# Attention and a two-of-eight expert layer on one core: one tag per token, a wait gone from the row scatters, and VectorE's low halves one position on

## The chip, the cores and the metric

The kernel runs on one core of a Trainium2 chip. The metric is the device time of one execution in microseconds, and less is better. The engines are named TensorE (PE in the profile), VectorE (DVE), ScalarE (ACT), GpSimd (POOL) and SyncE (SP, which here only issues transfers). Each engine runs its own instructions in the order in which they are written, and waits on semaphores for the others.

## The reference, cut to what matters

Eight sequences of 512 tokens with 256 channels pass an attention block, and the 4096 tokens then pass a shared feed-forward network and two of eight expert networks each.

```python
x = layernorm(x + attention(x))                    # 16 heads of 16, causal, q and k normed and rotated
normed = x * rsqrt(mean(x*x) + 1e-8) * norm_weight
shared = relu(normed @ sw1 + sb1) @ sw2 + sb2      # 256 -> 1024 -> 256
probs = sigmoid(normed @ router_w.T)               # 8 experts
scores, idx = top_k(probs, 2)
w = scores / (sum(scores) + 1e-6)
routed = sum over the two chosen e of  w_e * (relu(normed @ ew1[e] + eb1[e]) @ ew2[e] + eb2[e])
x = layernorm(x + shared + routed)
```

## The kernel before

**Two halves.** The first half runs a schedule of positions g from -33 to 209. A sequence c takes 20 positions more than the one before; tables of offsets (`QN`, `NAT`, `PROJ`, `NORMS`, `XN_ROWS`, `SCATTER` and others) say at which position of its sequence a piece of work stands, and `due(offsets, g)` lists what stands at g. Every engine has its own `step(g)`, which fixes the order inside a position. Nothing reorders anything: the tables and the lines of `step` are the order. The second half runs 39 routed tiles and 10 late tiles of the shared network.

**The attention part.** TensorE makes q, k and v (L1511), GpSimd rotates halves (`swap`, L629 and L632) and copies the normed q and k (`nat_high` L641, `nat_twice` L648 and L649), VectorE does the rest around these (`summed` L1069, `normed` L1084, `nat_low` L1094). TensorE computes scores (L1480), ScalarE exponentiates (L806), TensorE multiplies by v (L1502) and turns the result back (`NAT`, L1632, into the PSUM bank `mb`). VectorE then divides by the row sums (`averaged`: L1102 reads the sums, L1103 divides, and with that `mb` is free for the next `NAT`). `PROJ` (L1644) is the output projection, `added` (L1121) the residual, `norms` and `shifted` (L658 to L668 and L688 on GpSimd) the norms, `normalised` (L1143 to L1147) splits the normed rows into an fp16 high and low part in `xnh`.

**Routing.** `chosen` finds each token's two experts, `ranked` the row that each copy of the token gets in the list `xg_rows`, sorted by expert. Then GpSimd scatters: `scatter(c, t, k)` sends the 128 rows of tile t of sequence c to their row for the first (k = 0) or second (k = 1) expert with one indirect transfer (L679). Each row carries a tag in a column of `xnh`, written right ahead by a memset (L677), that tells row and k; the tag of k = 1 overwrites that of k = 0, so `scatter` with k = 1 waits until the four transfers with k = 0 have landed. There are 64 scatters, eight per sequence.

**Early tiles.** Six tiles of 256 tokens of the shared network (`N_EARLY`) are done at positions 161 to 206, beside the last sequence. A tile m has two hidden halves (`H`, L1564) and two output halves (`O`, L1601). ScalarE applies the ReLU of a hidden half at the next position (`early_hidden`, L861 and L865), VectorE makes its low half `hh` at the second next (`early_low`, L1271), and GpSimd adds a bias to the residual rows in `rs` (L709). `early_out` (L1293) writes the tile.

**From the first half to the second.** `tables` computes for every routed tile its expert and its first row. SyncE waits until every scatter has landed and then gathers the rows of tiles 0 and 1 (L520). `turn_rows` on TensorE (L1584) transposes a gathered tile, `turned` on VectorE (L1280) copies it to `xgT`; both stand ahead of the last early output half. ScalarE gathers every later tile (`load_rows`, L944); that of tile 2 stands behind the store of the last early tile (L882). Tile 2 is transposed ahead of the hidden product of tile 1.

**Routed tiles.** TensorE does a hidden product (L1705, 48 matmuls) and an output product (L1721, 48 matmuls) per tile. GpSimd computes from the tags where each row goes (`known`, two small operations), and scatters the results to `y_tok` (L734). Ten additions `pre_add` (L740) stand between these, for tiles 3, 7, ... 27, 28, 31 and 34; SyncE stores their results, and after the last store it loads residual rows (L551) and then rows of `y_tok` (L560) for the end.

## Time and profile before

| | us |
|---|---|
| median of 3 runs | 999.18 |
| lowest, highest | 998.37, 1002.56 |
| the profiled execution | 1000.01 |
| its span in the trace | 998.3 |
| TensorE busy in the span | 911.2 |
| GpSimd, VectorE, ScalarE busy | 433.5, 600.1, 624.2 |

Times in the trace are counted from the start of the span. A bracket at the end of a row tells how long the engine was idle before it and what ended that. "xN" at the end of a row of the timeline means N equal instructions in a row, told as one piece. The spans of GpSimd are rough. By the trace, attention alone lasts until about 387 us, the early tiles until 478 us, the routed tiles until about 887 us, and the late tiles until the end.

### The profile page before, as it was taken

The page shows a single profiled execution, that of the slowest core. Times are in us where ns is not written, and L with a number is a line of the kernel's source. Part 1 is how long each engine was busy: PE and PEld are TensorE (multiplying, and loading weights), DVE is VectorE, ACT ScalarE, POOL GpSimd, SP SyncE. Part 2 cuts the span into 40 slices and gives each one's busy share as a digit, 9 for nine tenths or more (in the row PEclk, how much of TensorE's full clock was granted, in tenths as well). Part 3 has the DMA queues.
Part 4 walks back from the last instruction along what each step waited for, and adds up shares of the span by engine and source line. Part 5 has one row for each costly group of instructions (what it writes and reads, how often), then busy time and mean ns, then how long its engine had stood idle before and what let it go on. Part 6 is the DMA issues. An engine that isn't in the chain of part 4 may idle for free.

```text
span 998.3 us, 26472 instructions
## 1 busy us (share of the span) xinstructions
PE 911.2 (91%) x9048; PEld 694.1 (70%) x9049; DVE 600.1 (60%) x1185; ACT 624.2 (63%) x1023; POOL 433.5 (43%) x637
## 2 busy tenths in 40 slices
PE   4589999997988987989899999999999999999995
PEld 1244555554554644877799899899999988688884
DVE  6756799888888855666234444444443332238875
ACT  3489898887888875434446655655654554556753
POOL 4654556877767654464024233432413233212211
PEclk9899999999999999999999999999999999999998
DMA  6011323434323255376882121221212121157641
GB/s 209 22 64 64 117 96 102 133 107 150 107 86 119 97 206 206 104 278 215 280 264 94 43 75 47 70 65 52 75 44 73 49 80 56 40 153 241 203 158 43
DMA packets 69539, 116.98 MB, mean 117 GB/s; under 512 B 7792, under 2 KB 45808, under 8 KB 69328
## 3 DMA queue, kind: packets, MB, share of 16 engines
q1 hardware_dynamic: 52080, 81.51, 24.7%
q10 hardware_dynamic: 10896, 16.40, 5.6%
q0 software_dynamic: 6480, 17.97, 5.0%
q8 instruction: 51, 0.84, 0.4%
q14 instruction: 32, 0.26, 0.1%
HBM read 68.67 MB, written 47.18 MB: 116 GB/s over the span
## 4 chain that ended last, share of the span: by engine, by line
PE 59%; POOL 14%; DVE 9%; issue 7%; ACT 5%; DMA 4%; ACTq 0%; SPq 0%; POOLq 0%; DVEq 0%
PE hb L1705 24%; PE yb L1721 23%; DMA xg_rows<-xnh,sl_i 3%; PE pv_bank L1502 3%; POOL xg_rows L679 3%; POOL nat L641 2%; PE ma L1511 2%; ACT prob L806 2%; PE tr L1584 2%; POOL rsum L632 1%; PE slot L1480 1%; POOL nat L648 1%; POOL nat L649 1%; POOL rsum L629 1%; POOL y L688 1%
## 5 line engine op out<-in xcount | busy, mean ns | idle before, releaser
L960 ACT ACTIVATE hf<-hb,b 128x256 f32<-128x256 f32 (+1 forms) x392 | 154.7, 456 | 228.0 <-PE hb L1705 224.2
L1705 PE MATMUL hb<-xgT,wts 128*128 128x256 f16 (+1 forms) x1872 | 219.8, 264 | 2.6 <-ACT hf L960 2.1
L1361 DVE TENSOR_TENSOR hh<-hf,hh 128x1024 f16<-128x1024 f32 (+1 forms) x98 | 118.7, 1211 | 168.6 <-ACT hh L965 130.4
L1721 PE MATMUL yb<-wts,hh 128*128 x1704 | 215.3, 273 | 0.1
L1705 PEld LDWEIGHTS hb<-xgT,wts 128*128 x1872 | 178.3, 98 | 25.3 <-issue 3.9
L734 POOL DMA_INDIRECT y_tok<-yb,dest x71 | 73.6, 1037 | 272.7 <-DVE yb L1373 255.2
L1721 PEld LDWEIGHTS yb<-wts,hh 128*128 128x128 f16 x1704 | 166.5, 98 | 21.8 <-issue 0.6
L806 ACT ACTIVATE prob<-slot 128x1024 f32<-128x1024 f32 x160 | 162.2, 1043 | 30.2 <-PE slot L1489 29.0
L965 ACT ACTIVATE hh<-hf 128x1024 f16<-128x1024 f32 (+1 forms) x98 | 97.6, 996 | 3.1
L1511 PE MATMUL ma<-wqkv,xTh 128*128 128x512 f16 (+1 forms) x384 | 79.7, 356 | 17.4 <-DVE xTh L1030 10.3
L1480 PE MATMUL slot<-stk 64*128 64x128 f16 (+3 forms) x512 | 63.5, 306 | 19.3 <-ACT prob L806 9.4
L679 POOL DMA_INDIRECT xg_rows<-xnh,sl_i x64 | 72.9, 1139 | 17.9 <-POOL xnh L677 14.1
L1502 PE MATMUL pv_bank<-prob,vst 128*32 128x512 f32 (+3 forms) x1024 | 76.5, 440 | 1.1 <-ACT prob L806 1.1
L1373 DVE SCALAR_TENSOR_TENSOR yb<-yb,b2bc 128x512 f32<-128x512 f32 (+1 forms) x39 | 25.1, 644 | 81.2 <-PE yb L1721 77.1
L1511 PEld LDWEIGHTS ma<-wqkv,xTh 128*128 128x128 f16 x384 | 38.4, 105 | 43.3 <-issue 24.1
L1502 PEld LDWEIGHTS pv_bank<-prob,vst 128*32 128x32 f32 x1024 | 30.1, 110 | 46.0 <-issue 39.1
L1489 PE MATMUL slot<-mask_b,ident_b 128*128 128x256 bf16 (+1 forms) x320 | 56.7, 260 | 0.0
L1705 PE MATMUL hb<-xgT,wts_s 128*128 128x256 f16 x480 | 54.0, 273 | 0.0
L1721 PE MATMUL yb<-wts_s,hh 128*128 128x256 f16 x480 | 53.9, 273 | 0.0
L1480 PEld LDWEIGHTS slot<-stk 64*128 64x128 f16 x512 | 17.2, 94 | 48.6 <-issue 21.0
L1721 PEld LDWEIGHTS yb<-wts_s,hh 128*128 128x128 f16 x480 | 47.0, 98 | 5.4
L1705 PEld LDWEIGHTS hb<-xgT,wts_s 128*128 128x128 f16 x480 | 47.0, 98 | 5.4
(197 smaller groups left out, 1422.6 us busy)
## 6 DMA issues: line engine op xcount, KB each, us to landing
wts<-in_w_all SPq DMA_DIRECT2D x19, 512.0 KB
stage<-in_w_all SPq DMA_DIRECT2D x16, 512.0 KB
w_split<-chunk_hl SPq DMA_DIRECT2D x16, 512.0 KB
wts<-y_tok SPq DMA_DIRECT2D x32, 256.0 KB, 4.6
xg<-xg_rows ACTq DMA_DIRECT2D x30, 264.0 KB
wts<-w_split SPq DMA_DIRECT2D x3, 2048.0 KB
xTf<-in_xT SPq DMA_DIRECT2D x8, 512.0 KB, 3.6
xin<-in_x SPq DMA_DIRECT2D x8, 512.0 KB, 4.3
```

What stands on the lines that cost most here:

```text
L679: pool.indirect_dma_start(a["xg_rows"], bass.IndirectOffsetOnAxis(ap=sl_i[:, c % 2, t, k:k + 1], axis=0), xnh[:, c % 2, t, :], None).then_ ...
L734: pool.indirect_dma_start(a["y_tok"], bass.IndirectOffsetOnAxis(ap=dest[:, slot, j:j + 1], axis=0), yb[:, par, j, :], None).then_inc(S(f"y ...
L806: act.activation(dst, src, ACT.Exp, scale=ATT_SCALE).then_inc(S("exp_done"), 1)
L960: act.activation(hf[:, c, 0:size], hb[c // 2][:, (c % 2) * TT:(c % 2) * TT + size], ACT.Relu, bias=bias, scale=1.0 / WS).then_inc(S("relu_ ...
L965: act.activation(hh[:, par, 0, cs, 0:size], hf[:, cs, 0:size], ACT.Copy).then_inc(S("h_hi"), 1)
L1361: dve.tensor_tensor(hh[:, par, 1, cs, 0:size], hf[:, cs, 0:size], hh[:, par, 0, cs, 0:size], ALU.subtract).then_inc(S("h_lo"), 1)
L1480: pe.matmul(slot[:, 512 * x + col:512 * x + col + T - P * j], stk[rows, par, 1, pr, P * j:P * j + P], stk[rows, par, 0, pr, P * j:T], star ...
L1489: last = pe.matmul(out, ident_b[:], mask_b[:, 0:diag[0], :], start=False, stop=True, skip_group_check=True)
L1502: last = pe.matmul(pv_bank[32 * r:32 * r + 32, P * j:T], vst[:, c % 2, j, 4 * g + r, :], prob[:, g % 2, r, SEG[j]:SEG[j] + T - P * j], sta ...
L1511: last = pe.matmul(out, xTh[:, c % 2, x, k, P * t:P * t + P], wqkv[:, y, k, cols], start=(n == 0), stop=(n == len(pieces) - 1))
L1705: ins = pe.matmul(hb[hc // 2][:, (hc % 2) * TT:(hc % 2) * TT + size], weights(e, c, w, hc * P, P), xgT[:, par, x * DC + c, 0:size], start= ...
L1721: ins = pe.matmul(ybank[par][:, j * D:(j + 1) * D], hh[:, par, x, hc, P * j:P * j + P], weights(e, DC + hc * D // CH, w, hc * D % CH, D), ...
```

## The change

**Tags.** The tag no longer depends on k. One operation per sequence writes the tags of all four tiles (`tile_f` plus 512 c) ahead of its first scatter, the 64 memsets are gone, and so is the wait of k = 1 for the transfers of k = 0. VectorE writes the token's second expert into the row (one copy in `chosen`). `known` compares that with the tile's own expert and adds 4096 where they are equal: four small operations instead of two. The tile's expert comes to all partitions by one matmul (`ones_r`, `te_h`) and one copy (`e_all`).

**VectorE's order.** `early_low` stands one position later, and inside the position behind `averaged`, `added` and `normalised`. The earlier offsets `XN_ROWS_LAST` now also hold for the last but one sequence.

**Around tile 1.** `turn_rows` and `turned` of tile 1 stand behind the last early output half instead of ahead of it.

**GpSimd's tail.** The loops over routed tiles are written out; `pre_add` now stands at tiles 3, 7, ... 35 and behind the last scatter.

```diff
-TB_OPS = 30
+TB_OPS = 31
 def rows_due(g):
-    return due(XN_ROWS, g) if g < NPOS * (NB - 1) + XN_ROWS_LAST[0] else [
-        (NB - 1, u) for u, off in enumerate(XN_ROWS_LAST) if NPOS * (NB - 1) + off == g]
+    return [(c, u) for c in range(NB) for u, off in enumerate(XN_ROWS if c < NB - 2 else XN_ROWS_LAST) if NPOS * c + off == g]
...
                 def scatter(c, t, k):
-                    if k == 0:
+                    if k == 0 and t == 0:
                         pool.wait_ge(S("slots_ready"), c + 1)
-                    landed = 2 * NT * (c // 2) + NT * k
-                    if landed:
-                        pool.wait_ge(S(f"scattered{c % 2}"), 16 * landed)
-                    pool.memset(xnh[:, c % 2, t, 2 * D:2 * D + 1], float(P * (k * NTILE + NT * c + t))).then_inc(S("tagged"), 1)
-                    pool.wait_ge(S("tagged"), TAGGED.index((c, t, k)) + 5)
+                        if c >= 2:
+                            pool.wait_ge(S(f"scattered{c % 2}"), 16 * TOPK * NT * (c // 2))
+                        pool.tensor_scalar(xnh[:, c % 2, :, 2 * D], tile_f[:], float(T * c), None, ALU.add
+                                           ).then_inc(S("tagged"), 1)
+                        pool.wait_ge(S("tagged"), c + NT + 5)
                     pool.indirect_dma_start(
...
-                def known(h, i):
+                def known(i):
-                    pool.tensor_tensor(dest_f[:, par, 0:nj], xg[:, par, 0:nj, 2 * D], xg[:, par, 0:nj, 2 * D + 1], ALU.add
+                    number, line, second = (xg[:, par, 0:nj, 2 * D + n] for n in range(3))
+                    moved, found = dest_f[:, par, 0, 0:nj], dest_f[:, par, 1, 0:nj]
+                    pool.tensor_scalar(moved, second, e_all[:, i:i + 1], float(NTOK), ALU.is_equal, ALU.mult
                                        ).then_inc(S("dest_known"), 1)
-                    wait_apart(pool, S, "dest_known", h * 4 + 2 * par + 1)
-                    pool.tensor_copy(dest[:, slot, 0:nj], dest_f[:, par, 0:nj]).then_inc(S("dest_known"), 1)
+                    pool.tensor_tensor(found, number, line, ALU.add).then_inc(S("dest_known"), 1)
+                    pool.wait_ge(S("dest_known"), 4 * i + 2)
+                    pool.tensor_tensor(found, found, moved, ALU.add).then_inc(S("dest_known"), 1)
+                    pool.wait_ge(S("dest_known"), 4 * i + 3)
+                    pool.tensor_copy(dest[:, slot, 0:nj], found).then_inc(S("dest_known"), 1)
...
+                for i in range(N_ROUTED):
                     if i + 2 <= R_LAST:
-                        known((i + 2) // 2, i + 2)
-                    scatter_output(i // 2, i)
-                    k = (i - LOOP_END) // 3 + (LOOP_END - 4) // 4 + 1
-                    if (i - LOOP_END) % 3 == 0 and k < N_LATE:
-                        pre_add(k, 16 * (k // 2 + 1))
+                        known(i + 2)
+                    scatter_output(i)
+                    if i % 4 == 3:
+                        pre_add(i // 4)
+                pre_add(N_LATE - 1)
...
 VectorE, chosen, ranked, tables:
+                    dve.tensor_copy(xnh[:, c % 2, :, 2 * D + 2], ixf[:, :, 1]).then_inc(S("ixf_done"), 1)
+                    dve.wait_ge(S("ixf_done"), 2 * c + 2)
+                    tb(dve.tensor_scalar(te_h[:], te[:, 0, :], float(NE - 1), None, ALU.min), False)
 VectorE, step:
                     for kind, m, q in early_due(g - 2):
-                        if kind == "H":
-                            early_low(m, q)
-                        elif q == 1:
+                        if kind == "O" and q == 1:
                             if m == N_EARLY - 1:
                                 turned(0, 0)
+                                dve.wait_ge(S("counted"), 2)
+                                dve.tensor_copy(e_all[:], mc[:, 0:N_ROUTED]).then_inc(S("tb"), 1)
+                            early_out(m)
+                            if m == N_EARLY - 1:
                                 turned(0, 1)
-                            early_out(m)
...
                     for c, u in rows_due(g):
                         normalised(c, u)
+                    for kind, m, q in early_due(g - 3):
+                        if kind == "H":
+                            early_low(m, q)
...
 TensorE, turn_rows and step:
-                        pe.wait_ge(S("tb"), 1)
+                        pe.wait_ge(S("tb"), TB_OPS + 1)
                             if m == N_EARLY - 1 and q == 1:
                                 turn_rows(0, 0)
+                                pe.wait_ge(S("tb"), TB_OPS)
+                                pe.matmul(mc[:, 0:N_ROUTED], ones_r[:], te_h[:], start=True, stop=True).then_inc(S("counted"), 1)
+                            early_output(m, q)
+                            if m == N_EARLY - 1 and q == 1:
                                 turn_rows(0, 1)
-                            early_output(m, q)
```

VectorE where the last sequence's divisions meet the first early tile: L1143 to L1147 are `normalised` of the last but one sequence, L1102 and L1103 a division, L1271 a low half. Before:

```order
L1271 TENSOR_TENSOR hh<-hf,hh 128x1024 [waits h_hi,xn_lo]
L1143 SCALAR_TENSOR_TENSOR xnf<-y,vv,ffn_nw 128x256 [waits x1_done,scattered0]
L1143 SCALAR_TENSOR_TENSOR xnf<-y,vv,ffn_nw 128x256 [waits x1_done]
L1146 CAST xnh<-xnf 128x2x256 [waits xnf_done]
L1147 TENSOR_TENSOR xnh<-xnf,xnh 128x2x256 [waits xn_hi]
L1102 RECIPROCAL rcp<-mb 128x16 [waits nat_done,xn_lo]
L1103 TENSOR_TENSOR an<-mb,rcp 128x256 [waits rcp_done]
```

The same place now, where the low half is L1275:

```order
L1143 SCALAR_TENSOR_TENSOR xnf<-y,vv,ffn_nw 128x256 [waits x1_done,scattered0]
L1143 SCALAR_TENSOR_TENSOR xnf<-y,vv,ffn_nw 128x256 [waits x1_done]
L1146 CAST xnh<-xnf 128x2x256 [waits xnf_done]
L1147 TENSOR_TENSOR xnh<-xnf,xnh 128x2x256 [waits xn_hi]
L1102 RECIPROCAL rcp<-mb 128x16 [waits nat_done,xn_lo]
L1103 TENSOR_TENSOR an<-mb,rcp 128x256 [waits rcp_done]
L1275 TENSOR_TENSOR hh<-hf,hh 128x1024 [waits h_hi]
```

The rows and the first division no longer stand behind the low half, which waits for ScalarE (`h_hi`).

GpSimd at the scatters of the last sequence, before, from its third one on (pairs of a memset and a transfer; the first two pairs have k = 0, the last one shown is the first with k = 1):

```order
L709 TENSOR_TENSOR rs<-rs,b2s 128x512 [waits e_res_in0]
L677 MEMSET xnh 128x1 [waits scattered1,slots_ready]
L679 DMA xg_rows<-xnh,sl_i 36608x528 [waits tagged]
L677 MEMSET xnh 128x1 [waits scattered1,slots_ready]
L679 DMA xg_rows<-xnh,sl_i 36608x528 [waits tagged]
L677 MEMSET xnh 128x1 [waits scattered1]
L679 DMA xg_rows<-xnh,sl_i 36608x528 [waits tagged]
```

All scatters of the last sequence now:

```order
L679 TENSOR_SCALAR xnh<-tile_f 128x4 [waits scattered1,slots_ready]
L682 DMA xg_rows<-xnh,sl_i 36608x528 [waits tagged]
L682 DMA xg_rows<-xnh,sl_i 36608x528
L712 TENSOR_TENSOR rs<-rs,b2s 128x512 [waits e_res_in0]
L682 DMA xg_rows<-xnh,sl_i 36608x528 x6
L712 TENSOR_TENSOR rs<-rs,b2s 128x512 [waits e_res_in1]
```

The memsets and every wait between the last six transfers are gone.

TensorE at the end of the first half, before:

```order
L1584 MATMUL tr<-keep_ident,xg 128x128 [waits mb_free,gathered0]
L1584 MATMUL tr<-keep_ident,xg 128x128 x7
L1584 MATMUL tr<-keep_ident,xg 128x128 [waits tb,gathered1]
L1584 MATMUL tr<-keep_ident,xg 128x128 x7
L1601 MATMUL yb<-wts_s,hh 128x256 x24
```

and now:

```order
L1592 MATMUL tr<-keep_ident,xg 128x128 [waits mb_free,gathered0]
L1592 MATMUL tr<-keep_ident,xg 128x128 x7
L1690 MATMUL mc<-te_h,ones_r 128x39 [waits tb]
L1609 MATMUL yb<-wts_s,hh 128x256 x24
L1592 MATMUL tr<-keep_ident,xg 128x128 [waits tb,gathered1]
L1592 MATMUL tr<-keep_ident,xg 128x128 x7
```

The last early output half no longer waits for the rows of tile 1.

## Rows read from the trace of the kernel before

**Rows 1.** Windows, first routed tiles: stretch, busy us of each engine, clock, DMA share, GB/s.

```profile
500.00:600.00 100.00, 100.00 (x953) 90.02 (x952) 45.43 (x45) 56.24 (x100) 32.84 (x38) 1.00 0.36 116
```

**Rows 2.** Timeline of TensorE: projection L1644 of sequences 0 to 2 and 5.

```profile
113.85 1.47 PE L1644 MATMUL mb<-wproj,aT 128*128 128x256 f16 x12
...
157.01 1.47 PE L1644 MATMUL mb<-wproj,aT 128*128 128x256 f16 x12
...
203.02 1.47 PE L1644 MATMUL mb<-wproj,aT 128*128 128x256 f16 x12
...
340.24 1.47 PE L1644 MATMUL mb<-wproj,aT 128*128 128x256 f16 x12
```

**Rows 3.** Timelines of VectorE, GpSimd and TensorE in one period, 224 to 250 us.

```profile
224.20 1.22 DVE L1094 TENSOR_TENSOR nat<-qn,nat 128x512 f16<-128x512 f32 x1 [1.94 <-POOL nat L641]
...
231.72 0.68 DVE L1094 TENSOR_TENSOR nat<-qn,nat 128x512 f16<-128x512 f32 x1
...
236.61 0.69 DVE L1069 TENSOR_TENSOR rsum<-rot,rsum 128x512 f32<-128x512 f32 x1 [1.67 <-POOL rsum L632]
...
232.24 0.10 POOL L677 MEMSET xnh<- 128x1 f16 x1 [1.52 <-DMA xg_rows<-xnh,sl_i]
...
233.98 0.62 POOL L648 COPY nat<-nat 128x512 f16<-128x512 f16 x1
...
231.95 0.63 PE L1632 MATMUL mb<-ident_f,raw 128*128 128x128 f32 x4 [2.19 <-DVE an L1103]
...
249.37 0.62 PE L1527 MATMUL mc<-keep_ident,nat 128*128 128x128 f16 x8 [0.82 <-DVE lg L1153]
```

**Rows 4.** Timelines of ScalarE, VectorE and TensorE where the early tiles begin.

```profile
393.05 1.06 ACT L865 ACTIVATE hh<-hf 128x1024 f16<-128x1024 f32 x1
...
394.20 1.23 DVE L1271 TENSOR_TENSOR hh<-hf,hh 128x1024 f16<-128x1024 f32 x1 [6.96 <-issue]
...
398.30 1.09 PE L1632 MATMUL mb<-ident_f,raw 128*128 128x128 f32 x4 [4.75 <-DVE an L1103]
399.19 3.72 PE L1564 MATMUL hb<-xgT,wts_s 128*128 128x256 f16 x24
...
407.43 2.78 PE L1601 MATMUL yb<-wts_s,hh 128*128 128x256 f16 x24
```

**Rows 5.** Timelines of GpSimd and SyncE: the last scatters and the first gathers.

```profile
454.37 0.98 POOL L679 DMA_INDIRECT xg_rows<-xnh,sl_i  x1 [0.28 <-DMA xg_rows<-xnh,sl_i]
...
461.18 0.10 POOL L677 MEMSET xnh<- 128x1 f16 x1 [4.42 <-DMA xg_rows<-xnh,sl_i]
...
465.62 1.94 POOL L679 DMA_INDIRECT xg_rows<-xnh,sl_i  x1 [0.28 <-issue]
...
470.04 1.79 SPq L520 DMA_DIRECT2D xg<-xg_rows  x2
```

**Rows 6.** Timelines of TensorE and ScalarE's queue: from the early to the routed tiles.

```profile
463.18 8.02 PE L1601 MATMUL yb<-wts_s,hh 128*128 128x256 f16 x72
...
475.11 0.62 PE L1584 MATMUL tr<-keep_ident,xg 128*128 128x128 f16 x8 [1.59 <-DMA xg<-xg_rows]
...
478.18 5.40 PE L1705 MATMUL hb<-xgT,wts 128*128 128x256 f16 x48
486.59 1.03 PE L1584 MATMUL tr<-keep_ident,xg 128*128 128x128 f16 x8 [3.01 <-DMA xg<-xg_rows]
...
480.48 0.43 ACTq L944 DMA_DIRECT2D xg<-xg_rows  x1
```

**Rows 7.** Timelines of GpSimd, SyncE and VectorE: an addition, then the late tiles' loads.

```profile
841.68 1.27 POOL L740 TENSOR_TENSOR rs<-rs,b2s 128x512 f32<-128x512 f32 x1
...
886.91 2.92 SPq L551 DMA_DIRECT2D wts<-resid  x6
894.55 6.34 SPq L560 DMA_DIRECT2D wts<-y_tok  x12
...
898.72 1.80 DVE L1399 SCALAR_TENSOR_TENSOR wts<-wts,keep_weights 128x256 f32<-128x256 f32 x4 [3.44 <-DMA wts<-y_tok]
```

64 lines of the change are left out of this document (31 added, 33 removed).

## The prediction, made before the changed kernel was run

> **What bounds the kernel now.** I read the windows of the span first. In the routed tiles TensorE is busy for all of 100 us [rows 1], in two matmul stretches per tile, so nothing the change does to the other engines there can shorten it. The late tiles run the same way. What can move lies before the first routed product. There I read the timeline of TensorE for its waits and went from each wait to the engine that ended it, and from there back in time.
>
> Three places come out. First, attention: a sequence's period. The projection starts at 113.85, 157.01 and 203.02, and three periods after that at 340.24 [rows 2]: periods of 43.16, 46.01 and three of 45.74 on average. The first has no scatter in it; the next four have eight each. In one of them TensorE waits 2.19 us for a division and 0.82 for the router's values, both VectorE's, while VectorE waits 1.94 and 1.67 us for GpSimd, and GpSimd 1.52 us for the transfers of k = 0 to land [rows 3]. Second, the start of the early tiles: TensorE waits 4.75 us for a division that stands in VectorE's queue behind a low half, which itself waits for ScalarE until 394.1 [rows 4]. Third, the boundary to the routed tiles: TensorE waits for gathered rows twice near 475 and for 3.01 us at 486.59 [rows 5, 6].
>
> **The tags, in attention.** Removed per sequence: seven memsets of 0.10 us with the 0.28 us until the transfer may start, 0.38 each [rows 3, 5], and the wait of 1.52 us; the first memset is replaced by one small operation of about its size. Three of the memsets stand ahead of the wait, so the copy of GpSimd at 233.98 could start 1.52 + 4 x 0.38 = 3.0 us sooner, but it needs the low part that VectorE ends at 232.40 (231.72 + 0.68), so it gains 1.6 and what VectorE itself is early. One memset fewer stands ahead of the copy that VectorE awaits at 224.20: 0.4. Together the operation at 236.61 comes 1.6 + 0.4 = 2.0 us sooner, which fits its wait of 1.67 plus 0.4 [rows 3]. So VectorE gains a lead of 2.0 us in each period with scatters. TensorE can use it only where it waits for VectorE. In the first such period that is the 0.82 us and the 0.4: 1.2. In the other three the lead meets the waits of 2.19 and 0.82; at most they can come back to the 43.16 us of the period without scatters, 137.22 - 129.48 = 7.7 us. I take 4.8 of it, some 60%, because the last of them is partly bound by ScalarE's exponentials and the lead has to be built up first. Sum: 1.2 + 4.8 = **6.0 us**, between 0 and 8.9.
>
> VectorE's added copy into the row and GpSimd's four start-up memsets are of the size of the smallest operations; the first lies ahead of a TensorE that is busy with other work when the choice is made, the second before GpSimd's first real work. I cost both at nothing; without that cover they would cost at most 0.7 us a sequence, the length of a whole 128x512 operation [rows 3].
>
> A rule speaks against this part. The trace shows the same VectorE operation (L1094) at 1.22 us at 224.20, while GpSimd copies, and at 0.68 at 231.72, in the very stretch in which GpSimd waits [rows 3]. The Trainium skill, "SBUF — State Buffer", section "Who interferes with whom", says that a VectorE instruction with two SBUF inputs contends with a GpSimd instruction that reads SBUF, and that the later one is held up entirely until the other is done. By that rule the removed wait was the time in which VectorE ran freely. What it would make of the time is the first rival below.
>
> **The early tiles' start.** Now the rows (L1143 to L1147) and the division stand ahead of the low half. GpSimd has their input at about 390, VectorE needs 2.0 us for the rows and 0.7 for the division and is done at about 393, when ScalarE is still at work (393.05 + 1.06) [rows 4]. TensorE asks for the bank at 398.30 - 4.75 = 393.55, so the wait goes. With it goes the low clock behind it: 24 matmuls take 3.72 us at 399.19 and 2.78 at 407.43 [rows 4], the transposes 1.09 instead of 0.63 [rows 3, 4], 1.4 together. Sum 4.75 + 1.4 = **6.2 us**. What is late next: the second division waits for the low half, which ends at 395.4, and TensorE comes to it after 24 matmuls at about 396.6; 1.2 us of slack. If a division missed that, up to 2 us would return: between 4 and 7. The low halves moved on have takers two positions later (ScalarE reuses `hf`, TensorE's output half), and I cost the move at nothing. Around `normalised` of the last sequence one low half leaves the path and one enters it, 1.23 us each [rows 4].
>
> **The boundary.** The last six scatters go out back to back. From 454.37 five further issues of 0.98 to 1.94 us [rows 5] put the start of the last one at 459.3 to 464.1 instead of 465.62. From there to the gathers' issue are 4.4 us (470.04 - 465.62), and to the second landing another 5.1 (475.11 - 470.04) [rows 5, 6]: 468.8 to 473.6. All of this in the old times; the earlier start shifts TensorE and the scatters alike. TensorE ends 72 matmuls at about 471.1 [rows 6], transposes tile 0 (0.45), broadcasts the experts (0.1), does the last output half (24 matmuls, 2.6) and is at 474.3, when tile 1 is there. So the waits for tiles 0 and 1 go. But tile 2's gather, which stands behind the store of that half, follows its end by 2.3 us (480.48 - 478.18) and lands 6.1 later (486.59 - 480.48) [rows 6]: 474.3 + 2.3 + 6.1 = 482.7. TensorE has then done tile 0's hidden product (to 480.0) and waits 2.7 us. Before it went on at 486.59: **3.8 us** gained. If the gather landed in time, 6.5; if it met more of the weights' traffic, 1.
>
> **The routed tiles and the tail.** `known` grows by two operations, at most 0.62 us each like the copy in rows 3, 1.2 per tile. GpSimd is busy for 33 of 100 us [rows 1], so about 7 us per tile are free: nothing. The matmul that broadcasts the experts is counted. The last `pre_add` moves behind the last scatter, and SyncE's six residual loads stand behind its store: they lose their lead of 7.6 us (894.55 - 886.91), at first sight; an addition of 1.27 us, its store, and six loads now push the first `y_tok` rows, for which VectorE already waits 3.44 us, by 2 to 7.6 us [rows 7]. VectorE's next low half stands behind these rows, and ScalarE wants it about half a tile later, one stretch of 48 matmuls, 5.2 us [rows 6]. I take 0, at most 2.4.
>
> **Sum.** 6.0 + 6.2 + 3.8 = 16.0 us off the profiled execution's 1000.01: 984.0. The median of the runs is 0.8 lower, so **983**. With every part at its favourable bound it is 999.2 - 22.4 = 977; with attention at 0, the start at 4, the boundary at 1 and the tail at 2.4 it is 996.6.
>
> **Rivals.**
>
> *GpSimd's work lands on VectorE (0.17).* Freed of its wait, GpSimd's copies run into VectorE's operations that used to run alone, each longer by 1.22 - 0.68 = 0.54 us [rows 3]. Four of them per period take back the lead of 2.0. Then attention gives nothing: 999.2 - 10.0 = 989. This is the page's rule at work. For it: the two lengths. Against: much of GpSimd's freed time is spent in issuing transfers.
>
> *The queue takes the wait's place (0.09).* With no wait in the code, six or eight transfers stand in one queue, and GpSimd is held at the issue (one took 1.94 us in the last row of four [rows 5]). Then the change doesn't do what it says: attention 0 and the boundary 2: 991.
>
> *The lead is lost to a transfer (0.07).* Early tiles and routed tiles need weights and rows that come when they come. If one of them lands no earlier, TensorE waits there for all that it gained: 998 to 999. Against: in these stretches TensorE's waits are for engines and gathers [rows 4, 6].
>
> *The low halves come late (0.05).* Slower: if each of the 12 low halves comes a whole position later for ScalarE and TensorE, at 2.0 us a position ((478.18 - 387.24) / 45, the start of VectorE's wait being 394.20 - 6.96 [rows 4, 6]), that costs 24 us, less the 16: 1007. It decides as soon as a low half ends after TensorE asks for its output; by my count there are 2 us and more of room at each.
>
> **How the numbers follow.** The forecast case (977 to 988) has 0.62. About 0.5% is what a measurement of this kernel can tell from no change, so faster is below 994.2: 0.62 + 0.17 + 0.09 = 0.88. Same 0.07, slower 0.05. The range 976 to 992 takes in the forecast and the first two rivals.
>
> **What would show it.** Periods of L1644 below 45 us from the second one with scatters on, and no wait of VectorE at `summed`; no memset L677 and no wait of GpSimd for `xg_rows`; TensorE's wait of 4.75 us gone and the 24 matmuls behind it at 2.8; the last six scatters started within 5 to 10 us instead of 11.3 (465.62 - 454.37); one wait of 2 to 3 us ahead of tile 2's transposes; TensorE busy for 100 of 100 us in the routed tiles. I am wrong if the early part is no shorter than by 10 us in all, or if TensorE waits in the late tiles.

## The result, and the profile after

| | us |
|---|---|
| median before (18 runs, beside those of the changed kernel) | 998.21 |
| median after (18 runs) | 990.02 |
| ratio, 95% interval | 0.9919, 0.9904 to 0.9933 |
| the profiled execution after, its span | 990.25, 988.5 |

The change gains 8.2 us. The forecast was 983 us, a gain of about 16. The two spans differ by 9.8 us (998.3 and 988.5). Five stretches, cut at rows that both traces have, tell where:

| stretch | before | after | gained | forecast |
|---|---|---|---|---|
| start to the first projection | 113.85 | 112.16 | 1.7 | none |
| to the first hidden product of the early tiles | 273.40 | 272.30 | 1.1 | 6.0 |
| to their first output product | 20.18 | 14.61 | 5.6 | 6.2 |
| to tile 2's transposes | 79.16 | 77.43 | 1.7 | 3.8 |
| to the end | 511.7 | 512.0 | -0.3 | 0 |

The first line can't be put down to the change. In the runs below, the three kernels with the start-up of before reach the first projection at 112.1 to 114.4, the nine with that of after at 109.2 to 113.3: one start-up varies by 4 us, and an effect of a microsecond or two on it is neither shown nor excluded. Without this line the spans differ by 8.1; the medians differ by 8.2.

**Attention.** The timeline of TensorE in the trace of after answers [rows 2], and the wait is the one of [rows 3]:

```profile
112.16 1.47 PE L1652 MATMUL mb<-wproj,aT 128*128 128x256 f16 x12
...
155.32 1.47 PE L1652 MATMUL mb<-wproj,aT 128*128 128x256 f16 x12
...
201.02 1.47 PE L1652 MATMUL mb<-wproj,aT 128*128 128x256 f16 x12
...
230.17 0.63 PE L1640 MATMUL mb<-ident_f,raw 128*128 128x128 f32 x4 [2.51 <-DVE an L1103]
```

The period without scatters is 43.16 as before. The four with scatters are 45.70, 46.07, 45.24 and 44.53 (before: 46.01, 46.81, 46.04, 44.37): 1.7 us gained in all, of which the rest of the stretch, from 336.86 to the early tiles, lost 0.6 (47.60, before 47.01). The wait for the division has not shrunk (2.19 before, 2.51 now). The timelines of GpSimd and VectorE in the same period tell what stands ahead of it:

```profile
206.94 1.17 POOL L661 TENSOR_TENSOR vv<-vv,keep_mhalf 128x2 f32<-128x2 f32 x1 [4.06 <-DVE vv L1131]
...
218.46 1.70 POOL L691 TENSOR_SCALAR y<-y,vv 128x256 f32<-128x256 f32 x2
220.33 1.10 POOL L682 DMA_INDIRECT xg_rows<-xnh,sl_i  x1 [0.18 <-issue]
221.45 0.62 POOL L644 CAST nat<-qn 128x512 f16<-128x512 f32 x1
...
230.68 1.13 POOL L651 COPY nat<-nat 128x512 f16<-128x512 f16 x1 [1.17 <-DVE nat L1094]
...
211.44 0.69 DVE L1121 SCALAR_TENSOR_TENSOR y<-mb,xin 128x512 f32<-128x512 f32 x1 [0.17 <-PE mb L1652]
...
222.11 1.22 DVE L1094 TENSOR_TENSOR nat<-qn,nat 128x512 f16<-128x512 f32 x1 [1.78 <-POOL nat L644]
...
233.83 0.69 DVE L1069 TENSOR_TENSOR rsum<-rot,rsum 128x512 f32<-128x512 f32 x1 [0.67 <-POOL rsum L635]
```

GpSimd's wait for `xg_rows` is gone and its copy (230.68) now waits for VectorE, as the forecast had it. VectorE's wait at `summed` went from 1.67 to 0.67; the forecast's sign was none. But all of this comes after the division. Ahead of it VectorE still waits 1.78 us for a cast (1.94 before, [rows 3]), which stands in GpSimd's queue behind the norms and two scatters.

**Where the early tiles begin.** TensorE, VectorE and GpSimd; the rows before are [rows 4]:

```profile
384.46 2.79 PE L1572 MATMUL hb<-xgT,wts_s 128*128 128x256 f16 x24
...
395.10 0.63 PE L1640 MATMUL mb<-ident_f,raw 128*128 128x128 f32 x4 [1.29 <-DVE an L1103]
...
399.07 2.78 PE L1609 MATMUL yb<-wts_s,hh 128*128 128x256 f16 x24
...
391.34 2.99 DVE L1275 TENSOR_TENSOR hh<-hf,hh 128x1024 f16<-128x1024 f32 x1 [2.02 <-ACT hh L865]
...
390.97 0.96 POOL L682 DMA_INDIRECT xg_rows<-xnh,sl_i  x1 [0.30 <-issue]
391.96 1.28 POOL L712 TENSOR_TENSOR rs<-rs,b2s 128x512 f32<-128x512 f32 x1
```

The wait of 4.75 us is gone, and so is the low clock behind it. A smaller one has come at the next division (1.29), since the low half ahead of that took 2.99 us instead of 1.23, while GpSimd issued a transfer and added the bias (which of the two it was is settled below, with e3_wait_back).

**The boundary.** TensorE, ScalarE's queue, GpSimd and SyncE's queue; before, [rows 5, 6]:

```profile
456.26 8.02 PE L1609 MATMUL yb<-wts_s,hh 128*128 128x256 f16 x72
...
467.42 0.61 PE L1592 MATMUL tr<-keep_ident,xg 128*128 128x128 f16 x8
...
476.50 0.69 PE L1592 MATMUL tr<-keep_ident,xg 128*128 128x128 f16 x8 [3.23 <-DMA xg<-xg_rows]
...
457.78 0.48 ACTq L846 DMA_DIRECT2D rs<-resid  x1
462.43 7.97 ACTq L882 DMA_DIRECT2D resid<-yb  x2
471.40 0.40 ACTq L944 DMA_DIRECT2D xg<-xg_rows  x1
...
467.95 1.26 POOL L712 TENSOR_TENSOR rs<-rs,b2s 128x512 f32<-128x512 f32 x1 [14.25 <-DMA rs<-resid]
...
456.19 1.52 SPq L520 DMA_DIRECT2D xg<-xg_rows  x2
...
458.23 31.12 SPq L528 DMA_DIRECT2D wts<-in_w_all  x13
```

Tiles 0 and 1 are there in time. From the 72 matmuls to tile 2's transposes it is 20.2 us, where it was 23.4 (486.59 - 463.18 in [rows 6]). Tile 2 is waited for 3.23 us, 0.5 more than forecast. Its gather goes out 3.8 us after the last output half (464.79 + 2.79 = 467.58), where 2.3 was forecast: the store ahead of it waited for a bias addition (467.95), and that for residual rows asked for at 457.78. The DMA view of this stretch gives 10.1 us for that load, and 3.5 in before. The last six scatters, from 444.30 to 451.37, started within 7.1 us, inside the 5 to 10 that were forecast.

The rest of the stretch gives 1.5 us back. The windows of after show TensorE's granted clock (the third number from the end) behind its waits of 2.23 and 1.83 us at 431 and 439, and its timeline the product that it made longer:

```profile
430.00:440.00 10.00, 6.68 (x76) 5.29 (x77) 6.85 (x39) 1.64 (x3) 4.36 (x6) 0.80 0.95 309
440.00:450.00 10.00, 10.00 (x81) 8.44 (x80) 9.31 (x29) 5.32 (x10) 7.97 (x7) 0.86 0.83 292
```

```profile
438.88 7.07 PE L1572 MATMUL hb<-xgT,wts_s 128*128 128x256 f16 x48
```

The clock was 0.50 from 440 to 442 and full again from 444, so that only a part of the product ran at the low level. The same product took 5.40 in before (at 447.47), behind the same two waits: 1.7 us lost. The 24 matmuls between the two waits took 4.45 us in after and 4.32 in before, and 2.78 where the clock is full.

**Routed and late tiles.** The windows of after, against [rows 1]; and SyncE's loads and VectorE's wait at the late tiles, against [rows 7]:

```profile
500.00:600.00 100.00, 100.00 (x957) 90.02 (x956) 45.61 (x45) 56.42 (x99) 41.26 (x56) 1.00 0.27 85
```

```profile
886.99 7.29 SPq L560 DMA_DIRECT2D wts<-y_tok  x12
...
893.47 1.80 DVE L1407 SCALAR_TENSOR_TENSOR wts<-wts,keep_weights 128x256 f32<-128x256 f32 x4 [7.94 <-DMA wts<-y_tok]
```

GpSimd is busy for 41.26 us instead of 32.84 in 100, and TensorE still for all of them. VectorE waits 7.94 us for `y_tok` instead of 3.44. TensorE doesn't wait longer for it: from 860 on it waits 0.6 us, for ScalarE (1.1 before).

### The profile page after: what moved, and what is told of

It reads as the page before. It is cut to its first block, busy times and chain, and to the rows that moved or that the text cites. A ratio compares the mean times of both kernels' runs of the same rounds, so it can differ in the third digit from the quotient of the medians.

```text
span 988.5 us, 26272 instructions
## 1 busy us (share of the span) xinstructions
PE 909.2 (92%) x9049; PEld 694.6 (70%) x9050; DVE 602.9 (61%) x1196; ACT 622.8 (63%) x1023; POOL 472.3 (48%) x664
## 4 chain that ended last, share of the span: by engine, by line
PE 63%; POOL 12%; DVE 10%; issue 7%; ACT 7%; DMA 1%; ACTq 0%; POOLq 0%; DVEq 0%
PE hb L1716 24%; PE yb L1732 24%; PE pv_bank L1510 3%; PE yb L1609 3%; ACT prob L806 2%; PE ma L1519 2%; POOL xg_rows L682 2%; PE hb L1572 2%; POOL nat L644 2%; PE tr L1592 1%; PE slot L1488 1%; POOL nat L651 1%; POOL rsum L632 1%; POOL vv L661 1%; PE slot L1497 1%
## 5 line engine op out<-in xcount | busy, mean ns | idle before, releaser
L744 POOL DMA_INDIRECT y_tok<-yb,dest x71 | 77.2, 1088 | 234.8 <-DVE yb L1381 224.5
L682 POOL DMA_INDIRECT xg_rows<-xnh,sl_i x64 | 74.4, 1162 | 16.2 <-issue 13.9
## 6 DMA issues: line engine op xcount, KB each, us to landing
wts<-in_w_all SPq DMA_DIRECT2D x19, 512.0 KB, 4.8
stage<-in_w_all SPq DMA_DIRECT2D x16, 512.0 KB, 4.4
w_split<-chunk_hl SPq DMA_DIRECT2D x16, 512.0 KB, 3.0
xTf<-in_xT SPq DMA_DIRECT2D x8, 512.0 KB, 3.9
xin<-in_x SPq DMA_DIRECT2D x8, 512.0 KB, 4.1
```

Source lines behind the costliest of these rows:

```text
L682: pool.indirect_dma_start(a["xg_rows"], bass.IndirectOffsetOnAxis(ap=sl_i[:, c % 2, t, k:k + 1], axis=0), xnh[:, c % 2, t, :], None).then_ ...
L744: pool.indirect_dma_start(a["y_tok"], bass.IndirectOffsetOnAxis(ap=dest[:, slot, j:j + 1], axis=0), yb[:, par, j, :], None).then_inc(S(f"y ...
```

## The experiments

All ratios are to the kernel before, run beside them; the rest is from the profiled execution of each. The columns are the stretches of the first table (from the first projection P to the first hidden product H, the first output product O, tile 2's transposes T and the end), then P to the end. Line numbers of a variant are one or a few off those of after.

| kernel | median | ratio, 95% interval | P to H | H to O | O to T | T to end | P to end |
|---|---|---|---|---|---|---|---|
| before | | | 273.4 | 20.2 | 79.2 | 511.7 | 884.5 |
| after | 990.02 | 0.9919, 0.9904 to 0.9933 | 272.3 | 14.6 | 77.4 | 512.0 | 876.3 |
| e1_tags_alone | 994.49 | 0.9966, 0.9942 to 0.9989 | 273.4 | 22.3 | 75.2 | 512.2 | 883.2 |
| e2_order_alone | 990.31 | 0.9910, 0.9875 to 0.9944 | 273.0 | 13.1 | 80.5 | 512.3 | 878.9 |
| e3_wait_back | 987.01 | 0.9883, 0.9844 to 0.9921 | 272.7 | 13.1 | 75.4 | 512.2 | 873.4 |
| e4_later | 978.24 | 0.9804, 0.9757 to 0.9851 | 267.1 | 13.6 | 71.9 | 511.3 | 863.8 |
| e5_weights_after | 985.06 | 0.9868, 0.9847 to 0.9889 | 272.3 | 14.6 | 74.0 | 510.4 | 871.3 |
| e6_turn_first | 989.46 | 0.9891, 0.9866 to 0.9916 | 274.6 | 14.6 | 74.4 | 510.8 | 874.4 |
| e7_gather_first | 985.86 | 0.9863, 0.9843 to 0.9884 | 272.4 | 14.6 | 74.0 | 510.3 | 871.4 |
| e8_best | 977.20 | 0.9792, 0.9769 to 0.9815 | 266.8 | 13.7 | 73.3 | 510.5 | 864.3 |
| e9_before_later | 999.50 | 1.0004, 0.9979 to 1.0028 | 272.5 | 22.2 | 78.6 | 512.5 | 885.8 |
| e10_two_moved | 987.85 | 0.9899, 0.9869 to 0.9930 | 273.0 | 13.9 | 71.9 | 511.0 | 869.8 |

The product that took 7.07 us in after took 5.40 in before, e3, e4, e6, e9 and e10, and 7.07 in e1, e2, e5, e7 and e8. The runs on either side share no edit; it is 1.7 us of the column O to T. The 24 matmuls ahead of it vary too: 2.78 us in e1, e4, e9 and e10, 3.94 in e6, 4.26 in e3, 4.32 in before, and 4.45 in the others. Counted at the full clock for both (an estimate: the column less what each took above 5.40 and 2.78), O to T is 77.6 in before, 74.1 in after, 73.6 in e1, 77.2 in e2, 73.9 in e3, 71.9 in e4 and e10, 70.7 in e5 and e7, 73.2 in e6, 69.9 in e8 and 78.6 in e9. The column P to H is good to some 2 us where a single trace is held against another: e6 has the program of after there and stands 2.3 above it.

### The two parts apart

e1_tags_alone is after with VectorE's order of before:

```diff
-    return [(c, u) for c in range(NB) for u, off in enumerate(XN_ROWS if c < NB - 2 else XN_ROWS_LAST) if NPOS * c + off == g]
+    return due(XN_ROWS, g) if g < NPOS * (NB - 1) + XN_ROWS_LAST[0] else [
+        (NB - 1, u) for u, off in enumerate(XN_ROWS_LAST) if NPOS * (NB - 1) + off == g]
...
                     for kind, m, q in early_due(g - 2):
-                        if kind == "O" and q == 1:
+                        if kind == "H":
+                            early_low(m, q)
+                        elif q == 1:
...
-                    for kind, m, q in early_due(g - 3):
-                        if kind == "H":
-                            early_low(m, q)
```

> The common tags, `known` on the expert and the new order at the boundary, with VectorE's low halves and the rows of the last two sequences where they stood before. The two traces put 5.6 us of the change's gain at the start of the early tiles (from the first hidden product to the first output product 20.18 us before, 14.61 after). If the parts simply add, this kernel keeps what the tags bring in attention (some 1.7 us in four periods) and at the boundary (3.2 us): 4 to 6 us faster than the kernel before, ratio about 0.995, with TensorE's wait of about 4.75 us for the division back. By the forecast's own terms (6.0 + 3.8) it would be 10 us faster, ratio 0.990.

e2_order_alone is before with the opposite of that diff.

> The kernel before with VectorE's new order alone: low halves behind the division, one position on, and the rows of sequence 6 at the places of sequence 7. Forecast 6.2 us, the traces showed 5.6 for the same stretch: 4 to 6.5 us faster than before, ratio about 0.9945. If the early tiles' wait can only go together with the tags (because GpSimd is late with the rows' input otherwise), it is within 1 us of before.

Alone, the order gains about what the whole change does (0.9910), and the tags 3.4 us (0.9966, 3.4 = 0.0034 x 998); expected were 4 to 6.5 us of the order and 4 to 6 of the tags. By the medians the parts don't add: 9.0 and 3.4 us alone, 8.1 together (0.0090, 0.0034 and 0.0081 x 998), and whether the tags bring anything on top of the order is not shown, for the interval of 0.9910 contains that of 0.9919. The traces add up roughly: 884.5 - 878.9 = 5.6, 884.5 - 883.2 = 1.3, and 8.2 for the whole change; with the clock taken out as above 7.3 and 1.4, together 8.7, against 9.9. The columns show where each part works. In attention the tags bring nothing or little (273.4 with them, 273.4 without; 272.3 and 273.0 with the new order). In H to O the order alone has 7.05 us (20.18 - 13.13), more than the 6.2 forecast, and the tags lose 2.2 us with the old order and 1.5 with the new (14.61 - 13.13). In the trace of e1 TensorE waits longer than ever for its division, since the low half ahead of the rows and of that division took 2.87 us; VectorE's timeline, then TensorE's:

```profile
389.53 2.87 DVE L1276 TENSOR_TENSOR hh<-hf,hh 128x1024 f16<-128x1024 f32 x1 [6.96 <-ACT hh L866]
...
395.27 1.09 PE L1640 MATMUL mb<-ident_f,raw 128*128 128x128 f32 x4 [6.39 <-DVE an L1104]
```

### The wait put back in attention

```diff
                         pool.wait_ge(S("tagged"), c + NT + 5)
+                    if k == 1 and t == 0 and c < NB - 1:
+                        pool.wait_ge(S(f"scattered{c % 2}"), 16 * (2 * NT * (c // 2) + NT))
```

> After, with GpSimd's wait for the four transfers of k = 0 put back ahead of the first transfer of k = 1 in sequences 0 to 6 (the tags stay common, the last sequence has no wait). It prices the removed wait in attention by itself. By the forecast's step (VectorE gains a lead of 2 us a period and TensorE can use most of it) the change would lose 4 to 6 us. By the reading of the two traces the wait lies behind the division that TensorE waits for, so that only the wait for the router's values comes back, some 0.8 us in each of three or four periods: 2 to 3 us slower than after.

Both expectations were wrong in sign: the median is 3 us below that of after, and though the intervals overlap, a loss of 2 us or more is excluded by them. In attention the wait costs 0.4 us (272.7 against 272.3), less than single traces can tell apart. In H to O it gains 1.5. Sequence 6's wait falls there, and while GpSimd stands in it, VectorE's low half takes 1.23 us; VectorE's and GpSimd's timelines in e3:

```profile
391.92 1.23 DVE L1277 TENSOR_TENSOR hh<-hf,hh 128x1024 f16<-128x1024 f32 x1 [1.96 <-ACT hh L867]
...
396.92 0.96 POOL L684 DMA_INDIRECT xg_rows<-xnh,sl_i  x1 [5.61 <-DMA xg_rows<-xnh,sl_i]
```

So the first rival's mechanism is real, at one place: the same operation takes 2.99 and 2.87 us beside GpSimd's issue and addition and 1.23 beside an idle GpSimd, and TensorE pays for it. It is the addition that does it, not the issue. Beside issues alone a low half takes 1.21 to 1.23 us, in after for instance at 396.25 (the next issue is at 396.76), by the timelines of VectorE and GpSimd, and in e10 below at 389.82 beside an issue from 389.78 on:

```profile
396.25 1.22 DVE L1275 TENSOR_TENSOR hh<-hf,hh 128x1024 f16<-128x1024 f32 x1
...
395.50 0.96 POOL L682 DMA_INDIRECT xg_rows<-xnh,sl_i  x1 [0.30 <-issue]
```

Beside an addition (1.27 or 1.28 us when alone) one of the two is held: in e5 the low half at 428.48 takes 1.23 and the addition at 428.52 then 2.32; in e4 the addition begins at 385.15 and the low half at 385.50 takes 2.01. The Trainium skill, "SBUF — State Buffer", section "Who interferes with whom", says that a VectorE instruction with two SBUF inputs contends with a GpSimd instruction that reads SBUF, and that the later one is held up entirely. These two pairs agree with it. The pair in after does not, by its recorded starts: the low half (391.34) began 0.62 us ahead of the addition (391.96) and was the one held, until 1.09 us behind the addition's end (394.33 against 393.24). The recorded spans of GpSimd are rough, and whether its true start was earlier is open.

### The scatters moved to later positions

```diff
-SCATTER_2 = (64, 66, 67, 68)
+LATER = (61, 63, 64, 66)
+LATER_2 = (67, 68, 69, 70)
 def dispatch_position(c, t, k):
-    if k == 0:
-        return NPOS * c + SCATTER[t]
-    return NPOS * c + (SCATTER_2[t] if c < NB - 1 else SCATTER[-1])
+    if c < NB - 1:
+        return NPOS * c + (LATER, LATER_2)[k][t]
+    return NPOS * c + SCATTER[min(t + 4 * k, 3)]
```

> After, with the eight scatters of sequences 0 to 6 issued later (the first two from positions 58 and 59 to 61 and 63, the last at 69 and 70, where GpSimd idles for 2.97 us). New theory: a period is set by GpSimd's row of work between the variances and its first cast into `nat`, and the two issues in that row (1.10 us each, with 0.7 us of tag and waits) are what separates 46.07 us from the 43.16 of a period without scatters; then TensorE's wait of 2.4 us for the division shrinks by 2 us or so in each of four periods: 6 to 9 us faster than after, periods of 43.5 to 44.5. Rival, the collisions of GpSimd with VectorE at the ports: the same work still collides, only elsewhere: within 2 us of after, periods of about 46.

0.9804: 11.5 us less than after (0.0115 x 998), more than the 6 to 9 expected. Of the 12.5 us between the two traces, 5.2 lie in P to H, which is what was expected, 1.0 in H to O, 5.5 in O to T and 0.7 behind it; of the 5.5 some 3.3 are the clock, which was full at both places named above, 0.8 a shorter wait for ScalarE (1.45 for 2.23) and 1.5 the boundary. The mean granted clock was 0.980 to 0.990 in the six runs of e4 and 0.976 to 0.985 in the 18 of after, so that the clock is a part of the difference of the medians too. The four periods are 44.08, 44.49, 44.71 and 42.92, all but one below 44.5, and of TensorE's waits of 1.5 to 2.5 us for the division none is left. The timelines of GpSimd, VectorE and TensorE in e4, to be held against those of after:

```profile
215.85 2.03 POOL L692 TENSOR_SCALAR y<-y,vv 128x256 f32<-128x256 f32 x2
217.83 0.60 POOL L645 CAST nat<-qn 128x512 f16<-128x512 f32 x1
...
238.08 0.97 POOL L683 DMA_INDIRECT xg_rows<-xnh,sl_i  x1 [0.30 <-issue]
...
218.47 1.20 DVE L1095 TENSOR_TENSOR nat<-qn,nat 128x512 f16<-128x512 f32 x1 [0.42 <-POOL nat L645]
...
225.46 0.63 PE L1641 MATMUL mb<-ident_f,raw 128*128 128x128 f32 x4 [0.29 <-DVE an L1104]
```

The cast follows the norms directly, VectorE waits 0.42 us for it instead of 1.78, and the last two scatters (the second at 238.08) lie where GpSimd had idled. GpSimd does the same work (35.74 us busy in this period, 34.20 in that of after), and VectorE is busy for about as long (40.09 and 41.29). The rival, as it was put (the same work collides elsewhere, and the period stays), is out.

The next run asks whether the common tags are needed for it: before, with the same later positions and nothing else.

> The kernel before (tags, waits and VectorE's order as they were) with only the scatters of sequences 0 to 6 issued at the later positions. If the two issues ahead of GpSimd's first cast are the whole of what a scatter costs attention, the old tags and the old wait do not matter: periods of 44 to 45 us, ratio to before 0.990 to 0.994. If the common tags are what makes the later positions possible (the old wait for k = 0 would now stand in front of GpSimd's copies at the end of the period), the periods stay at 46 and the ratio is within 0.3% of 1.

1.0004: they are. The periods fell only to 44.75, 45.78, 44.44 and 45.84, with the old wait now in front of GpSimd's casts at the end of the period, and VectorE waits there, by the timelines of GpSimd and VectorE in e9:

```profile
236.56 0.10 POOL L678 MEMSET xnh<- 128x1 f16 x1 [1.52 <-DMA xg_rows<-xnh,sl_i]
...
246.63 0.69 DVE L1095 TENSOR_TENSOR nat<-qn,nat 128x512 f16<-128x512 f32 x1 [2.67 <-POOL nat L642]
```

And what little attention gained (0.9 us in P to H) went where the early tiles begin, 22.2 us instead of 20.2.

The last of this group moves only the two scatters that stand ahead of the cast:

```diff
+LATER = (61, 61, 61, 63)
...
     if k == 0:
-        return NPOS * c + SCATTER[t]
+        return NPOS * c + (LATER if c < NB - 1 else SCATTER)[t]
```

> After, with only the first two scatters of sequences 0 to 6 moved, from positions 58 and 59 to 61, behind the first cast of `nat`; the other six stay. If the row ahead of that cast is the whole matter, the periods come to 44.1 to 44.7 as with all eight moved, TensorE's wait for the division is gone and the ratio to before is 0.980 to 0.984. If what counts is how much GpSimd issues between the first cast and the next copies, the wait moves there: VectorE waits at its next low part of `nat` or at `summed`, and the ratio stays at 0.990 or above.

0.9899, at the rival's 0.990, and P to H is 273.0, no better than before: the four periods are 46.08, 46.59, 47.52 and 42.85. (The profiled execution was the fastest of ten, 981.5 against a median of 987.9, so its other stretches say little.) The row ahead of the cast is therefore not the whole matter. Three scatters now stand between the cast and GpSimd's next copies, and the waits are there, in the timelines of VectorE and TensorE:

```profile
227.22 0.69 DVE L1095 TENSOR_TENSOR nat<-qn,nat 128x512 f16<-128x512 f32 x1 [2.42 <-POOL nat L645]
...
232.67 0.69 DVE L1070 TENSOR_TENSOR rsum<-rot,rsum 128x512 f32<-128x512 f32 x1 [2.21 <-POOL rsum L636]
...
226.69 0.62 PE L1530 MATMUL ma<-keep_ident,nat 128*128 128x128 f16 x8 [2.12 <-POOL nat L653]
```

Read together, e4 and e10 say that no issue should stand ahead of a GpSimd result that somebody is waiting for; each issue takes 1.0 to 1.8 us. Which of e4's eight places matter most was not tried.

### The boundary

e5_weights_after holds the biases and the raw weights back until the residual rows have landed:

```diff
+                sp.wait_ge(S("e_res_in1"), 16 * (N_EARLY // 2))
                 sp.dma_start(b2bc[:], a["b2all"][0:NE, :].rearrange("e d -> (e d)").partition_broadcast(P)
```

> After, with SyncE's loads of the biases and of the raw weights held until the last early tile's residual rows have landed. In the trace of after these rows were asked for at 457.78 and had not come before 467.9, while the weights' loads ran from 458.2; in the trace of before they came in 3.5 us. If that is why the last output was stored 1.5 us late (3.8 us from the half's end to the gather of tile 2, where before had 2.3), TensorE's wait of 3.23 us for tile 2 shrinks to 1.7: 1 to 2 us faster than after. If the store is late for another reason, nothing changes; if the weights are then late, TensorE waits in the first routed tiles.

0.9868, 5 us less than after. The chain read off the trace was right and sized too low. In e5, on ScalarE's queue, GpSimd, SyncE's queue and TensorE:

```profile
455.71 0.48 ACTq L847 DMA_DIRECT2D rs<-resid  x1
...
467.64 0.40 ACTq L945 DMA_DIRECT2D xg<-xg_rows  x1
...
460.08 1.26 POOL L713 TENSOR_TENSOR rs<-rs,b2s 128x512 f32<-128x512 f32 x1 [8.40 <-DMA rs<-resid]
...
460.40 27.81 SPq L529 DMA_DIRECT2D wts<-in_w_all  x12
...
471.03 0.61 PE L1593 MATMUL tr<-keep_ident,xg 128*128 128x128 f16 x8
```

The residual rows are there after 4.4 us (460.08 - 455.71, no longer 10.1). The gather of tile 2 follows the output half, which ends at 462.72 + 2.79 = 465.51, by 2.1 us, and lands before 470.8, so that the whole wait of 3.23 goes. The expectation had counted the gather's earlier start (1.7 us) and not its landing in 3.2 us or less instead of 5.1. The first link is borne out by e3, where the loads are not held and happen to start 1.6 us behind the request for the residual rows (in after the biases' load goes out with it, at 457.75): these came in 3.7 us and the gather went out 2.1 us behind the half. Its landing took 6.4 us there, and TensorE waited 2.91. Of the kernels that don't hold the loads, only after shows the slow load of 10.1 us; e1, e3, e4, e6 and e10 have 2.9 to 3.7. How often it comes in the runs of after that were not profiled is open; that their medians differ is not (0.9868 and 0.9919, intervals apart). It also takes 1.6 us off the last stretch (512.0 to 510.4): without the wait the hidden product behind it runs at the full clock (in after 48 matmuls took 6.79 us at 477.48, where 5.40 is the full speed). No weights are missed.

e7_gather_first is e5 with the gather of tile 2 moved ahead of the store (only the new place is shown; the old one, behind the store, is taken out):

```diff
                         if kind == "O" and q == 1:
+                            if m == N_EARLY - 1:
+                                act.wait_ge(S("tb"), TB_OPS)
+                                load_rows(1, 0)
                             act.wait_ge(S("y_ready"), m + 1)
```

> As the run with the weights' loads held, and ScalarE asks for tile 2's rows ahead of the store of the last early tile, as soon as GpSimd has read tile 0's. The gather should go out some 4 to 5 us sooner and the wait of 3.23 us ahead of tile 2's transposes should go: 3 to 4 us faster than after. If the landing is what is slow (5.1 us from issue to landing, longer under the weights' traffic), 1 to 2 us of wait stay.

Same as e5 (0.9863 and 0.9868; 871.4 and 871.3 in the traces): with the first edit there was no wait left to take, though the gather went out some 2.6 us sooner (467.97 - 113.04 against 467.64 - 110.12, counted from P).

e6_turn_first puts tile 1's transposes and copy back ahead of the last output half.

> After, with tile 1's transposes and copy ahead of the last output half again, as before the change. The forecast let the half cover tile 1's landing. In the trace of after both tiles had been asked for at 456.19, 8 us ahead of tile 0's transposes, and no transpose waited, so the order should be worth nothing: within 1 us of after. If tile 1 lands late after all, a wait of 1 to 2 us stands ahead of its transposes.

0.9891 against 0.9919 for after, intervals overlapping. Its transposes of tile 1 now wait 0.86 us for the copy of the experts, not for a transfer, and tile 2 is waited for 1.38 us instead of 3.23. That stretch, from the 72 matmuls on, is 19.3 us and not 20.2: the new order at this place gains nothing once the tags are common, and may lose 1 us.

### A faster kernel

> The later scatters in attention, the weights' loads held and the gather of tile 2 ahead of the store, together. The later scatters alone gave a ratio of 0.980 to before; with 1 to 3 us more at the boundary: ratio 0.977 to 0.980, 975 to 978 us. If the boundary's waits are gone already with the later scatters (that run's trace shows 1.39 us for tile 0 and 0.21 for tile 2), nothing is added.

0.9792, 977.2 us: 13 us less than after. It is at one with e4_later within the intervals; since its product at 429.64 took 7.07 us and the 24 matmuls ahead of that 4.45, where e4 has 5.40 and 2.78, the traces put it some 2.8 us ahead at an equal clock (864.3 - 3.3 = 861.0 against 863.8). The medians don't show that. The view of TensorE's waits up to tile 2, engine, line and awaited first, then us in total, times and the longest, in before, after and e8:

```profile
PE mb L1632 <- DVE an L1103: 14.2, 8, 4.7
PE tr L1584 <- DMA xg<-xg_rows: 6.3, 3, 3.0
```

```profile
PE mb L1640 <- DVE an L1103: 10.5, 6, 2.5
...
PE tr L1592 <- DMA xg<-xg_rows: 3.2, 1, 3.2
```

```profile
PE slot L1491 <- ACT prob L808: 8.4, 13, 1.5
...
PE mb L1643 <- DVE an L1106: 2.3, 6, 0.5
```

The waits for the division are down from 14.2 us to 10.5 and 2.3, those for gathered rows from 6.3 to 3.2 and none; what is left most is TensorE's wait for ScalarE's exponentials.

## Why the prediction was right and wrong

The direction and the range (976 to 992) held, and the gain was half of what was forecast. That 990 lies inside the range is owed to the room left for the first two rivals. It lies next to the first rival's 989, and attention gave little, as that rival had it, but the reason was another. By its own steps:

- **Attention, 6.0 forecast, 1.1 measured.** The failed step is "TensorE can use it only where it waits for VectorE. ... In the other three the lead meets the waits of 2.19 and 0.82". The lead exists (VectorE comes 0.8 us sooner to `summed`, not 2.0), but it arises at 236.61 in the period of [rows 3], 4.7 us behind the wait of 2.19 at 231.95. To help that one it would have to last into the next period, and it doesn't. There GpSimd waits 4.06 us for VectorE's variances (206.94 above), and VectorE waits for TensorE's projection (211.44), so that each period's lead ends with it: that addition of GpSimd starts 5.92 us behind the projection in after (206.94 - 201.02), and started 5.85 behind it in before (208.87 - 203.02). It meets the wait of 0.82 alone, which is gone in after, and 0.74 is what the period of 46.81 lost. That wait should have been followed back in time from its own place: GpSimd's cast, the norms, the two issues. e4 shows that the 6 us were there to be had (6.3 in P to H), for moving the issues, with the tags as the condition (e9).
- **How large the removed wait was.** With the wait back (e3) attention lost 0.4 us. That GpSimd waits 1.52 us was read rightly; it was not on the path.
- **Start of the early tiles, 6.2 forecast, 5.6 measured.** Right in mechanism: the order alone gave 7.05, because the clock and both divisions came out well. The tags took 1.5 back. This is the term that the part on the tags priced at nothing outside attention, and the rival *GpSimd's work lands on VectorE* put into attention; it fell here instead, where a low half of 1.23 us met GpSimd's addition. The slack of 1.2 us at the second division, named in the forecast, was too small for it, within the "up to 2 us" allowed.
- **Boundary, 3.8 forecast, 3.2 measured.** The tiles 0 and 1 and the one wait for tile 2 came as told (3.23 for 2.7). Two sizes were off and partly cancelled: the gather went out 3.8 us behind the half instead of 2.3, and landed in 5.1 instead of 6.1. The first is a piece of the rival *The lead is lost to a transfer*: the earlier scatters let SyncE start the biases' and the weights' loads at once, and these slowed the residual rows that the last early output needs (holding them took it away, e5). The bound for a gather in time was also right: in e5 this stretch takes 16.84 us, 6.6 less than before, where 6.5 was stated. (By the forecast's own rows 486.59 - 482.7 is 3.9, not 3.8; that changes nothing.)
- **The clock.** The forecast counted what the clock gives back behind a removed wait (1.4) and not that at two other waits, near 431 and 439 in after, the matmuls behind each may lose up to 1.7 us or nothing (the second in six of twelve profiled executions); after lost 1.8 us more there than before.
- **Tail and routed tiles, 0 forecast, 0.3 lost.** GpSimd had the room for `known` and VectorE for the later rows: T to the end is 511.7 before and 510.3 to 512.5 in all others; the 1.6 us between after and e5 are mostly the clock behind tile 2 (6.79 - 5.43 = 1.4).
- **The other rivals.** *The queue takes the wait's place* did not happen: the issues stayed at 1.0 to 1.8 us (one of 2.34 at the end), GpSimd had 0.16 to 0.30 between them. *The low halves come late* did not either: no TensorE wait for a low half appeared.
- **How far "wrong if the early part is no shorter than by 10 us" served.** It was 10.1 us shorter, of which 1.7 were start-up, so that it was passed only with the start-up's help. A bound on a stretch has to begin behind the start-up.

## What to carry to other kernels

A wait that is removed helps another only if that one comes later in the same period, or if the lead survives the place where the engines synchronise again: so begin at the wait of the bounding engine and go back in time from there, and do not begin at the engine that is set free. Transfers issued by an engine that also computes are work of 1 to 2 us each in its queue; put them behind the results others wait for, and after removing a wait look anew where they should stand. A wait of one engine can also be what keeps it out of another's way: ask what work moves into the time that comes free, and beside which operation. When a chain of transfers becomes earlier, look what bulk load starts with it, and hold that load until the small transfers on the path have landed.

## What the hardware showed that was not expected

- The residual load of the last early tile, 256 KB, took 10.1 us in after, with a bias load of 1024 KB and weight loads of 512 KB each asked for from another queue within 0.5 us of it, and 2.9 to 4.7 us in the eleven other profiled executions, where these started 1.6 us behind it or later. The Trainium skill, "DMA: Bandwidth & Descriptors", section "Queues, rings and completion order", says that a DMA engine takes the queues in turn, a packet at a time. By that rule a small load is slowed by a large one on another queue, and the trace agrees in kind; it does not show the packets' turns.
- The same VectorE subtraction of 128x1024 took 1.23 us beside an idle GpSimd, 1.21 to 1.23 beside GpSimd's issues of indirect transfers, and 1.92 to 2.99 where its addition of 128x512 held it up. Taking away a wait of GpSimd (5.61 us long in e3) moved that addition beside the subtraction and cost TensorE 1.5 us there.
- Behind two waits of 1.4 to 2.2 us and 1.8 to 1.9 us the granted clock fell for a part of the next matmuls in some executions and not in others: the 48 behind the second took 7.07 us in six of twelve profiled executions and 5.40 in the others. Between e4 and e8, with the same two waits (1.45 and 1.86, 1.46 and 1.83), the program there differs in nothing that TensorE does, and the clock from 430 to 435 was 1.00 in the one and 0.66 in the other.
- The start-up varied by 4 us between kernels with the same start-up (first projection from 109.2 to 113.3), more than most effects studied here; only stretches that begin behind it could be compared.
